# A decoder layer: TensorE's order from a planner with needs, delays and a priority, and four groups' context products kept ahead in place of eight

## The reference

```python
x = x + linear_attention(layernorm(x))              # phi = elu + 1, causal sums, then Wo and bias
x = x + cross_attention(layernorm(x), ctx, ctx)     # softmax over 128 context tokens, no output weight
h = layernorm(x)
h = silu((h @ w1.T) * s1) * ((h @ w2.T) * s2)       # 256 -> 1024, ternary weights
h = gelu((h @ h1.T) * sh1)                          # 1024 -> 1024
h = gelu((h @ h2.T) * sh2)                          # 1024 -> 1024
x = x + (h @ w3.T) * s3                             # 1024 -> 256
```

## Time and profile before

| | us |
|---|---|
| median of 3 runs (lowest to highest) | 1114.05 (1111.82 to 1116.39) |
| the profiled execution | 1114.61 |
| its span in the profile | 1112.8 |
| TensorE busy in the span | 1068.1 (96%) |
| VectorE, ScalarE, GpSimd busy | 724.5 (65%), 523.7 (47%), 198.7 (18%) |

### The profile page before, as it was taken

The page is one execution under the profiler, slowest core; times in us unless marked ns, Lnnn a source line. Parts: engine busy times, 40 slices in busy tenths (PEclk is TensorE's granted clock), DMA queues, the critical chain, the costliest instruction groups (busy, mean ns, idle before and its releaser), DMA issues.

```text
span 1112.8 us, 24962 instructions
## 1 busy us (share of the span) xinstructions
PE 1068.1 (96%) x9962; PEld 883.0 (79%) x9962; DVE 724.5 (65%) x1644; ACT 523.7 (47%) x869; POOL 198.7 (18%) x267
## 2 busy tenths in 40 slices
PE   4889899999999999999999999999999999999997
PEld 4778777888788888888788887878888788878885
DVE  6576876567765777577766686656875667745411
ACT  2345353634537363554546364373635546363531
POOL 1222321012210132012210232102310113200300
PEclk9889999999999999999999999999999999999999
DMA  4348666435443554335533254234433244334642
GB/s 119 89 152 284 197 210 220 150 114 172 160 140 106 180 166 152 123 100 182 162 124 105 78 184 153 95 120 135 155 129 110 96 152 161 105 116 162 223 137 75
DMA packets 68004, 161.18 MB, mean 145 GB/s; under 512 B 7344, under 2 KB 22832, under 8 KB 67888
## 3 DMA queue, kind: packets, MB, share of 16 engines
q1 hardware_dynamic: 64432, 148.03, 40.2%
q10 hardware_dynamic: 3456, 11.54, 3.5%
HBM read 136.47 MB, written 34.60 MB: 154 GB/s over the span
## 4 chain that ended last, share of the span: by engine, by line
PE 89%; DVE 5%; issue 2%; ACT 2%; POOL 1%; DMA 1%; ACTq 0%; SPq 0%; DVEq 0%; POOLq 0%
PE bank L1071 41%; PE bank L1056 10%; PE bank L954 8%; PE bank L927 5%; PE bank L896 5%; PE bank L1091 5%; PE bank L911 4%; PE bank L901 3%; PE bank L872 2%; PE bank L1004 1%; PE bank L936 1%; POOL ctxs L544 1%; DVE att_l L786 1%; PE bank L947 1%; DVE mx L803 1%
## 5 line engine op out<-in xcount | busy, mean ns | idle before, releaser
L1071 PE MATMUL bank<-hidden_b,weight_ring 128*128 128x512 f32 x1024 | 253.6, 396 | 0.3
L1071 PE MATMUL bank<-hidden_a,weight_ring 128*128 128x512 f32 x1024 | 253.1, 397 | 0.0
L1071 PEld LDWEIGHTS bank<-hidden_a,weight_ring 128*128 128x128 f32 x1024 | 187.4, 189 | 38.5 <-issue 1.0
L1071 PEld LDWEIGHTS bank<-hidden_b,weight_ring 128*128 128x128 f32 x1024 | 186.1, 188 | 39.2 <-issue 1.6
L674 ACT ACTIVATE hidden_full<-bank,columns_sb 128x512 f32<-128x512 f32 x128 | 88.2, 689 | 217.7 <-PE bank L1071 217.5
L1056 PE MATMUL bank<-hidden_b,weight_ring 128*128 128x512 f32 x512 | 134.2, 402 | 0.1
L786 DVE TENSOR_TENSOR att_l<-bank,cst 128x512 f32<-128x512 f32 x128 | 83.6, 678 | 62.3 <-PE bank L954 62.2
L555 POOL TENSOR_TENSOR hidden_a<-hidden_full,hidden_a 128x512 fp32r<-128x512 f32 x64 | 84.1, 1314 | 168.3 <-ACT hidden_a L669 168.3
L529 POOL TENSOR_TENSOR ve<-mv,eps 128x1 f32<-128x1 f32 (+1 forms) x80 | 19.3, 241 | 529.2 <-DVE mv L689 529.2
L1056 PEld LDWEIGHTS bank<-hidden_b,weight_ring 128*128 128x128 f32 x512 | 92.3, 190 | 17.2 <-DMA weight_ring<-weights_scratch 0.5
L803 DVE TENSOR_REDUCE mx<-bank 128x4 f32<-128x512 f32 x128 | 83.7, 681 | 8.7 <-PE bank L954 8.5
(11 more groups left out here) (136 smaller groups left out, 1674.8 us busy)
## 6 DMA issues: line engine op xcount, KB each, us to landing
weight_ring<-weights_scratch SPq DMA_DIRECT2D x160, 512.0 KB, 3.4
weights_scratch<-in_h ACTq DMA_DIRECT2D x16, 512.0 KB, 5.0
xn3T_scratch<-hidden_b SPq DMA_DIRECT2D x16, 512.0 KB, 4.4
weight_bits<-in_h SPq DMA_DIRECT2D x32, 256.0 KB, 3.5
weight_ring<-weights_scratch SPq DMA_DIRECT2D x32, 256.0 KB, 2.7
x_in<-in_x SPq DMA_DIRECT2D x16, 256.0 KB, 5.0
xb<-in_x SPq DMA_DIRECT2D x16, 256.0 KB, 4.9
ctx_in<-in_ctxT SPq DMA_DIRECT2D x16, 256.0 KB, 3.3
```

The lines of the kernel that those rows point to most:

```text
L1071: mm = eng.matmul(pbank(step, g, n)[:, :], ring[:, slot, kk * P:(kk + 1) * P], src[:, part, kk, :], start=(kk == 0 and part == 0), stop=(k ...
```

## The change

`KEPT` becomes groups 1 to 4; groups 5 to 8 compute `xk` and `xv` within their own chain, like 9 to 15. The hand-made times are replaced by a planner. Each step keeps a number (`rank`, its old slot within a group plus 42 per group), which is now only a priority, and gets a duration per engine. `needs` lists for every step what must be done before it. A clock then runs through the program: each engine that is free takes a step that is ready. SyncE, GpSimd and VectorE take the lowest rank; ScalarE keeps to the table it has unless something has waited for `HOLD` = 1 us, and a change costs it 1.28; TensorE takes tiled steps while it is in a tiled mode, then plain steps, then tiled ones that are two or have waited `PATIENCE` = 5 us, then a quarter of the turn. A step of TensorE starts only if its banks are free (with `SPARE` = 1 left for the turn's tiles) and if what will empty them is held up by nothing else. The turns' own steps on the other engines have rank -1000. The matmuls and the other instructions within the steps are the same. `FILL` goes from 40 matmuls at three places to 104 at four.

```diff
-    KEPT = range(1, 9)
+    KEPT = range(1, 5)
+    NL, NX, NFULL = 5, 4, 3
+    SPARE, PATIENCE, HOLD = 1, 5.0, 1.0
...
-    TURN = 136.82
-    FF0 = 83.98
-    QUARTER = TURN / 88
-    EARLY = ((0.14, 1.15), (28, 0.94), (66, 1.3), (110, 1.88))
-    STRETCH = 2.2
-    JOIN = 1.47
...
+    def put(step, g, n=0, rank=0.0, took=None, **slots):
         for engine, t in slots.items():
+            tasks[engine, step, g, n] = (rank + t, took[engine])
+
+    PITCH = 42
...
+        steady("q", tensor=-7.66, scalar=-6.57, vector=-4.94, took=dict(tensor=1.42, scalar=.8, vector=1.45))
...
+            u = 60 + 6 * g
+            put("load_ctx", g, 0, u, sync=-50, took=dict(sync=5))
+            put("xk", g, 0, u, tensor=1, scalar=1, took=dict(tensor=1.42, scalar=.55))
...
+    FF = -1000.
...
+            put("xn3T", 2 * f + p, 0, FF, tensor=0, scalar=0, vector=0, took=dict(tensor=.44, scalar=.52, vector=.6))
...
+                    put("hidden", f, 4 * n + q, 0, tensor=0, took=dict(tensor=.91))
+            put("gelu", f, n, FF, scalar=0, took=dict(scalar=1.2))
...
+    LATE = {"tensor": .3, "vector": .15, "scalar": .15, "gpsimd": .2, "sync": 0}
+    AT = {("scalar", "split", n): (7, 7.7, 8.4, 15, 15, 15, 15)[n] for n in range(7)}
+    AT |= {("scalar", "copy_weights", j): 12 + 3.2 * j for j in range(NCH)}
...
+    while left:
+        upcoming = []
+        for engine in engines:
...
+                when = max([AT.get(key[:3] if key[1] in ("split", "copy_weights") else key, 0.0)]
+                           + [done[x] - LATE[engine] * (x[0] == engine) if x in done else 1e9 for x in prereqs[key]])
+                if when <= now:
+                    found.append((tasks[key][0], key, when))
...
+                    if want and (len(open_) < want + (0 if turn or not going else SPARE) or any(x not in done for x in held_up[entry[1]])):
+                        continue
...
+                patient = ff and all(now - e[2][2] < PATIENCE for e in tiled) and len(tiled) < 2
+                if mode and tiled:
+                    found = [tiled[0][2]]
+                elif plain:
+                    found = [plain[0][1]]
+                elif tiled and not patient:
+                    found = [tiled[0][2]]
+                else:
+                    found = ff[:1]
...
+            elif engine == "scalar" and found:
+                same = [e for e in found if e[1][1] not in (GELUS if table == "exp" else EXPS)]
+                old = [e for e in found if now - e[2] >= HOLD]
+                upcoming += [e[2] + HOLD for e in found if e[2] + HOLD > now]
+                found = [min(same)] if same else [min(old)] if old else []
+            elif found:
+                found = [min(found)]
...
+            done[key] = now + took + LATE[engine]
...
-                FILL = {("lin_scores", 0, 0): 18, ("lin_sums", 0, 0): 14, ("project", 0, 0): 8}
+                FILL = {("ln1T", 0, 0): 24, ("q", 0, 0): 20, ("xv", 0, 0): 40, ("lin_scores", 0, 1): 20}
```

More of the change, by code:

```diff
@@ L125, in decoder_layer_program @@
[L125 to L144 removed]
+            steady("lin_scores", b, tensor=-0.28 + 4.6 * b, took=dict(tensor=.95))
@@ new lines, in decoder_layer_program @@
+    bank_free, bank_last, holder = [0.0] * 8, [None] * 8, {}
+    mode, table, waiting = 0, "exp", 0.0
+    heads_of = {engine: [fam for fam in families if fam[0] == engine] for engine in engines}
+    at_ = {fam: 0 for fam in families}
+    left = sum(len(x) for x in families.values())
+    now, streak = 0.0, 0
+    prereqs = {}
+    for fam in families.values():
+        for key in fam:
+            prereqs[key] = [x for x in needs(*key) if x in tasks]
+    follows = {fam[i]: fam[i - 1] for fam in families.values() for i in range(1, len(fam))}
@@ new lines, in holds_up @@
+    def holds_up(key, task, depth=0):
+        below, others = False, []
+        for x in prereqs[key] + ([follows[key]] if key in follows else []):
+            reached, more = (True, []) if x == task else holds_up(x, task, depth + 1) if depth < 3 and x in prereqs else (False, [])
+            below, others = below or reached, others + (more if reached else [x])
+        return below, others
+    held_up = {("tensor", step, g, n): [x for u in uses_of(step, n) for x in holds_up(freed_by(step, g, u), ("tensor", step, g, n))[1]
+                                               if x[1] not in ("lin_sums", "x_sums", "gate", "hidden", "w3", "tanh", "gated", "gelu", "out") or x[2] < g]
+               for engine, step, g, n in prereqs if engine == "tensor"}
@@ new lines, in before @@
+    def before(engine, entry, step):
+        i = next(i for i, e in enumerate(program[engine]) if e[1:] == entry)
+        program[engine].insert(i, (program[engine][i][0], step, 0, 0))
+    before("vector", ("gelu_rest", NF - 1, 2 * KH - 6), "flag")
+    before("tensor", ("hidden", NF - 1, 8 * KH - 16), "flag")
+    place["flag", 0, 0] = place["hidden", NF - 1, 2 * KH - 4]
+    use_before["flag", 0, 0] = use_before["hidden", NF - 1, 2 * KH - 4]
+    use_before["hidden", NF - 1, 2 * KH - 4] = ("flag", 0, 0)
```

414 lines of the change are left out of this document (240 added, 174 removed).

## The result

The changed kernel takes **1118.49 us** (median of 20 runs) where the kernel before takes 1111.78 (20 runs, 1109.03 to 1116.39): a ratio of 1.0061, 95% interval 1.0049 to 1.0074. One of the 20 runs took 2674.98 us and is left out of the ratio. The change is 0.6% slower where the forecast had 1.3% faster. The profiled execution took 1120.39 us around a span of 1118.5. The page's shares say little by themselves: TensorE is at 96% in both.

What follows compares the result with a forecast made beforehand. TensorE's own work was taken to bound the steady turns, leaving ordering gains to the start. Savings of 17.2 + 2.0 less 2.6 and 1.4 made 15.2 us, from 1114.05 to 1099 us, range 1085 to 1114.

Steps and rivals of the forecast that it cites:

- both together would put the gate at 97 ... I take 90: Start: earlier group 1 statistics and a quicker last xn3T bring the first gate matmul from 123.25 to 90 us.
- saved 41.1 - 23.9 = 17.2 us: Start: TensorE time lost before the first gate matmul falls from 41.1 to 23.9 us, saving 17.2.
- rival 2: Start and turns: gate near 78 us and cheaper turns, 29 us saved, 1085 us; chance 0.11.
- rival 1: Start: earlier gate, turns as now, 1099 us, own range 1090 to 1108; chance 0.56.
- 4 x 0.64 = 2.6: Turns: four contexts moved there cost 3.54 us each against 2.9 back to back, 2.6 us dearer.
- 2 more runs of feed-forward per turn: Turns: 2 more interruptions at 0.10 us each over 7 turns, 1.4 us lost.
- rival 4: Turn seams: TensorE waits for ScalarE's or POOL's tiles; at 4 us a turn, 1127 us; chance 0.14.
- Rival 5: ScalarE: table loads dearer than the planned 1.28 us; at 4 us a turn at TensorE, 1127 us; chance 0.03.
- From the first gate to 257: After the first gate matmul, up to 257 us: fewer waits and less half clock save 2.0 us, bounds 0 and 4.
- The fills: Start: 104 fill matmuls in place of 40, taken as 0 together with the slow first projection's 1.3 us.
- a gate after 105: Start: a first gate matmul later than 105 us would show the prediction wrong; 80 to 100 was expected.
- 3 and 4 together: The third rival: gate stays late, past 105 us, giving 1108 to 1114 us; chance 0.16. The fourth: see rival 4.

Runs made afterwards that it cites:

- old_kept4: The kernel before, in its written order, with only KEPT set to groups 1 to 4 in place of 1 to 8: 1125.83 us, 1.0143.
- kept8: The changed kernel with KEPT back at groups 1 to 8, planner, prices and fills as they are: 1114.45 us, 1.0035.
- kept8_patient: The changed kernel with eight groups kept, PATIENCE 20 us, output store priced at 8 us and context load at 7: 1094.86 us, 0.9828.

## Why the prediction was wrong

**The step that failed** is "both together would put the gate at 97 ... I take 90", and with it the sum for the start, "saved 41.1 - 23.9 = 17.2 us". The gate came at 117.93 and the start saved 1.3. Both single facts under it held: the statistics moved by 18.3 us, and the end from ln3 to xn3T closed up by 5.8. But a gain at the head of a chain was carried to its end as if every later link waited for it alone. By the last ln3 nothing of the 18.3 was left (-1.2). What holds the end is the length of the two chains: they take 111 us even with group 2 barred and VectorE busy for 61%. At most 7 us more are group 2's work in their way. The prediction's own words against rival 2, "every group is one long chain across four engines", were right and were not applied to rival 1.

**The second step** is the price of the four contexts, "4 x 0.64 = 2.6". The 0.64 is the extra for interruptions. The forecast did put the contexts' whole time in its sum as work moved, and that is sound only if what is lost before the gate shrinks with it. It didn't: 48.1 lost with four, 41.1 with eight; old_kept4 shows the real price, 15 us in the written order, and under the planner it is 3 to 4 us as changed, 7 with patience alone (1.0002 against 0.9940) and 14 to 24 with patience and prices. All these pairs go the same way. Eight kept contexts do "pin" the start in that the gate of kept8 comes 10.7 us later, but 17.7 us more work lies before it, so 7 of them fill time that is otherwise lost.

**The turns.** I forecast 2 more runs of feed-forward per turn than the 34 to 38 of before (the trace has 31 to 37). There were 69 fewer in all (177 against 246), which was the cheap direction; with the contexts' price against it, -2.3 us is left in the ledger. What came in its place is rival 4's waits, +5.9 us of idle time after the gate, about 0.8 a turn and not the 4 that this rival needed alone; and half clock within turns, which no step of the prediction had (3.4 us lost in the profiled execution; in the mean execution half clock anywhere costs 2.8 to 4.5 us more than before). The seams that it named (tanh, gelu, table changes) were not where TensorE waited: the two waits with half clock behind them were for x2T behind the output store and for the gated product behind VectorE's low-bit test and oT.

**Rival 5** did not come about. There are 86 table loads in place of 52, each 1.28 us (one more stands at the start):

```profile
L803 ACT ACT_TABLE_LOAD x43 | 55.2, 1283 | 0.8
L768 ACT ACT_TABLE_LOAD x23 | 29.5, 1283 | 0.4
L716 ACT ACT_TABLE_LOAD x11 | 14.1, 1283 | 0.2
L722 ACT ACT_TABLE_LOAD x8 | 10.3, 1283 | 1.8 <-DVE qf L836 1.7
```

kept8_patient has 84 and is fast, so they are not what the change lost by. The Trainium skill ("ScalarE: Activation LUTs", What ACT_TABLE_LOAD costs) gives 1.28 plus a drain of 1.38; all 86 loads here agree with the first. The trace shows no such drain: at 943.91 a load begins right behind an activation that ended at 943.89 (the rows above), and in the median over the loads the next activation starts 12 ns behind them.

**From the first gate to 257** I had 2.0 saved, 4 at most. Idle time there is 0.9 us in place of 3.7, and of the two stretches at half clock one stayed (118.0 to 121.5). That is 6.8 us lost before and 2.6 now, 4.2 saved: right in kind and undersized.

**The fills** were put at 0; 0 to 1.5 us saved was measured, which can't be told from 0.

**The sum again**, from the profiled pair: start 1.3 saved; idle after the gate 5.9 lost; half clock after the gate 2.0 lost (10.2 us of busy time at half clock in place of 6.2); the rest of TensorE's work after the gate, contexts and runs together, 0.9 saved. That is 5.7 lost, as the spans differ; the medians differ by 6.7. The medians also hold the clock's part, and how the difference divides in the mean execution is not shown. The forecast's own sign of being wrong, a gate after 105, came true. By rivals it is 3 and 4 together: the gate stayed late *and* the turns got waits. I had given them 0.16 and 0.14 as if one excluded the other.

**Left open**: how much of the 3 to 24 us between four and eight kept groups is the fixed cost and how much the plan drawn. The planner's results scatter by 10 us for changes of one number, more than the 6.7 us that the change lost, and a handful of plans of each kind is too few to average that away. What is clear of it is the distance to the forecast: 19.5 us, 16 of them in the start.

## What to carry to other kernels

Count useful work against time lost before a milestone, not the milestone's place: here the kernel with the earliest gate (111 us) was among the slowest and the five that beat the kernel before had theirs at 125 to 133. A gain at the head of a chain is worth what is left of it at the end, so look at each engine that the chain passes before carrying it over. A list scheduler whose clock is at hand can be asked first: this one had the gate at 111.4, not 90. Work that depends on nothing belongs in the gaps of the start. In an in-order list one step that waits at the head holds everything behind it, so transfers are best priced as they are under load; with eight groups kept that removed 18 us of ScalarE's waits, with four the priced plan was 5 us slower.

## What the runs showed of the hardware

- **A short wait in a dense turn can be followed by half clock.** TensorE's waits of 1.75 us (ended 424.74) and 2.51 us (ended 943.94) were followed by stretches of 3.4 us at 1.2 GHz, beginning at about 425.3 and 944.1, in turns in which it was busy for 98% (140.59 of 143.23) and 97% (93.02 of 96.24). Each costs about 1.7 us on top of the wait. The two waits thus cost 1.7 to 2 times their own length. A wait of 1.03 us, ended at 691.75, had no such stretch behind it.
- **Transfers take longer beside others.** x_in of group 1 was asked for at 9.67 us and there at 17.70, 8.0 us, while the page's median for x_in is 2.9. The output store's median is 5.9 us in the changed kernel where it was 3.5 before, with 8.1 at the place shown. The DMA engines are busy for 79% and 82% of these two stretches (second column from the right; over whole turns it is 37% to 45%):

```profile
9.67:17.70 8.03, 7.09 (x87) 6.88 (x84) 2.17 (x5) 1.61 (x5) 1.22 (x1) 1.00 0.79 281
935.09:943.20 8.11, 6.34 (x100) 5.43 (x98) 6.31 (x17) 1.85 (x3) 2.84 (x5) 1.00 0.82 282
```

From the view of the changed kernel's DMA issues (KB each, median us to landing):

```profile
x_in<-in_x SPq DMA_DIRECT2D x16, 256.0 KB, 2.9
...
ctx_in<-in_ctxT SPq DMA_DIRECT2D x16, 256.0 KB, 4.2
...
out_T<-residual SPq DMA_DIRECT2D x16, 256.0 KB, 5.9
```
